# Deformable-convolution sampling: the subtraction for the low part of the coefficients goes from VectorE to GpSimd, behind its tap six

## What is computed

```
off, mask = projections of a depthwise convolution      # per pixel, 8 groups x 9 points
value     = x @ vp_w.T + vp_b
sampled   = bilinear reads of value at (pixel + point + off)
out       = sum over the 9 points of mask * sampled     # per group of 16 channels
x         = x + out @ op_w.T
```

## Time and profile before

| what | value |
|---|---|
| time, median of 3 runs | 1475.63 us (1475.12 to 1478.64) |
| the profiled execution | 1483.07 us, its span 1481.3 us |
| TensorE busy over the span | 81% |
| VectorE busy over the span | 66% |
| ScalarE busy over the span | 51% |
| GpSimd busy over the span | 48% |
| mean granted TensorE clock | 0.901 |

### The profile page before, as it was taken

One profiled execution on the slowest core, in us unless ns is written; L12 is line 12 of the kernel. 1 busy time (PEld: TensorE's weight loads), 2 busy tenths in 40 slices (PEclk: granted clock), 3 DMA queues, 4 the chain that ended last, 5 costly groups with the idle time before them and its releaser, 6 DMA issues. The chain is left out here.

```text
span 1481.3 us, 41520 instructions
## 1 busy us (share of the span) xinstructions
PE 1193.9 (81%) x13483; PEld 782.1 (53%) x13484; DVE 974.0 (66%) x2318; ACT 753.3 (51%) x1960; POOL 703.6 (48%) x842
## 2 busy tenths in 40 slices
PE   3982699999999987789887888887841699999974
PEld 1541344444444432355655555555530599999973
DVE  4996898888898732366777776767626244444435
ACT  1222555554555416367675665666410377777750
POOL 2000478787887850001144354454657355555550
PEclk9996699999999989699999998999755699999995
DMA  3000000000000012121112121221201122222218
GB/s 125 0 0 12 1 1 1 0 0 0 0 0 0 1 28 87 37 48 39 35 40 53 49 54 36 66 55 33 82 27 50 45 67 68 67 68 68 68 55 334
DMA packets 67555, 66.63 MB, mean 45 GB/s; under 512 B 13135, under 2 KB 57167, under 8 KB 67175
## 3 DMA queue, kind: packets, MB, share of 16 engines
q1 hardware_dynamic: 56679, 43.14, 10.8%
q0 software_dynamic: 8448, 17.58, 3.6%
q10 hardware_dynamic: 2304, 4.20, 0.7%
HBM read 29.93 MB, written 23.00 MB: 36 GB/s over the span
## 5 line engine op out<-in xcount | busy, mean ns | idle before, releaser
L1627 ACT ACTIVATE a_E<-a_E,a_nm 128x96 f32<-128x96 f32 x512 | 148.5, 364 | 117.8 <-DVE a_nm L1768 117.3
L2128 ACT ACTIVATE e_hT<-e_ph,e_b 128x128 f32<-128x128 f32 x544 | 155.5, 369 | 74.1 <-PE e_ph L2085 74.1
L441 POOL TENSOR_TENSOR s_pc<-s_wide,VP 128x512 f32<-128x512 f32 x112 | 143.0, 1277 | 74.8 <-ACT s_wide L520 68.8
L674 PE MATMUL s_pbc<-s_AT,s_sel 120*128 120x512 bf16 x400 | 134.2, 386 | 31.7 <-ACT s_wide L520 16.9
L432 POOL TENSOR_TENSOR s_acc<-s_acc,s_pb 128x512 f32<-128x512 f32 x112 | 142.3, 1270 | 22.0 <-DVE s_pb L603 21.5
L685 PE MATMUL s_pout<-s_pa,s_opT 128*128 128x512 f32 x288 | 151.5, 607 | 0.0
L2096 PE MATMUL e_py<-e_shared,e_hT 128*128 x1088 | 150.4, 281 | 1.1 <-ACT e_hT L2128 1.1
L2085 PE MATMUL e_ph<-e_xT,e_w1s 128*128 128x128 f32 x1088 | 147.7, 280 | 0.5 <-DVE e_w1s L2157 0.4
L1386 POOL DMA_INDIRECT slots<-m_pay,m_pos x128 | 128.2, 1002 | 38.8 <-issue 38.4
L2066 POOL DMA_INDIRECT picks<-e_yw,e_rows x136 | 134.3, 987 | 22.6 <-POOL e_tick L2064 21.0
L2085 PEld LDWEIGHTS e_ph<-e_xT,e_w1s 128*128 128x128 f32 x1088 | 134.6, 195 | 1.9 <-issue 0.9
(11 more groups left out here) (228 smaller groups left out, 2436.0 us busy)
## 6 DMA issues: line engine op xcount, KB each, us to landing
a_V<-a_VT SPq DMA_DIRECT2D x176, 68.0 KB
e_rows<-slots SPq DMA_DIRECT2D x136, 66.0 KB, 1.8
c_y<-picks SPq DMA_DIRECT2D x16, 512.0 KB, 5.6
X<-in_x SPq DMA_DIRECT2D x8, 512.0 KB, 8.1
out<-c_o ACTq DMA_DIRECT2D x16, 256.0 KB, 5.4
picks<-e_yw,e_rows POOLq DMA_INDIRECT x136, 2.3
e_w<-in_w SPq DMA_DIRECT2D x1, 2048.0 KB, 7.4
slots<-m_pay,m_pos POOLq DMA_INDIRECT x128
```

Of the source, the lines that this page charges most:

```text
L441: nc.gpsimd.tensor_tensor(prod_c[k][:].rearrange("p (a b) -> p a b", a=HALF), wide[k][:].rearrange("p (a b) -> p a b", a=HALF), window(n, ...
L674: pe.matmul(p_bc[bank_of["spread", t]][:], sel[:, t % 5, :], AT[j][:, t // 5, :], start=True, stop=True).then_inc(bc, 1)
L1627: act.activation(E[t % 2][:, o, :], E[t % 2][:, o, :], ACT.Exp, bias=nm[:, t % 2, o:o + 1]).then_inc(powered, 1)
L2128: ins = act.activation(hT[j % 2][:, q, :], p_h[j % 2][:, q * P:(q + 1) * P], ACT.Gelu, bias=b1[:, bass.ds(e, 1), q:q + 1].rearrange("p o h ...
```

## The change

GpSimd makes the subtraction `split_low` instead of VectorE. In its queue it stands behind tap 6, that is behind b6 and ahead of c8. The one for chunk 0 stands ahead of all chunks on GpSimd. VectorE's next `split_rest`, which overwrites `s_rest`, gets a wait for `low` of the chunk before. Nothing else moves: `low` still releases TensorE's round 0 behind tap 8.

```diff
             def _(pool):
                 nc.gpsimd.memset(zero[:], 0.0).then_inc(zeroed, 1)
 
+                def split_low(c):
+                    pool.wait_ge(mid, c + 1)
+                    nc.gpsimd.tensor_tensor(parts[:, :, :, 2].rearrange("p t a w -> p a t w"), rest[:],
+                                            parts[:, :, :, 1].rearrange("p t a w -> p a t w"), ALU.subtract)\
+                      .then_inc(low, 1)
+
                 def chunk(c, j, n):
...
                                 window(n, j, t), ALU.mult).then_inc(mul_c, 1)
+                        if t == 6 and (not known(c) or c + 1 < NCH):
+                            split_low(c + 1)
+                split_low(0)
                 chunks(pool, chunk)
...
-                def split_low(c):
-                    dve.wait_ge(mid, c + 1)
-                    dve.tensor_tensor(parts[:, :, :, 2].rearrange("p t a w -> p a t w"), rest[:],
-                                      parts[:, :, :, 1].rearrange("p t a w -> p a t w"), ALU.subtract)\
-                       .then_inc(low, 1)
-
...
                             if t == 1:
+                                dve.wait_ge(low, c + 1)
                                 split_rest(c + 1)
-                            if t == 5:
-                                split_low(c + 1)
...
                 split_rest(0)
-                split_low(0)
                 for k in range(WEIGHT_STEPS):
                     weights(1, k)
```

## The result

The changed kernel is slower: 1491.44 us median of 5 runs (1487.31 to 1519.86) against 1476.03 us, a ratio of 1.0085 with a 95% interval of 1.0058 to 1.0112, some 12.5 us.

A forecast was written before the change was run, and what follows sets the result against it. The prediction took a chunk's period as TensorE's work plus one place where VectorE is late. It added 17 us of longer chunks and 9 us of clock, 26 us, for about 1501 us median, range 1485 to 1517.

The forecast's parts named there:

- Where it stands: GpSimd's queue: subtraction behind c5 and b6, so round 0 starts 3.2 us later, old waits vanish; chunk about 1.0 us longer.
- The duration: The subtraction of 800 elements on GpSimd, priced from two-input f32 additions: 1.95 us.
- the two old waits: TensorE's waits at the spreads of taps 10 and 11: said to vanish, giving back 2.2 us a chunk.
- The removed contention: VectorE loses its 1.18 us subtraction; `s_MY` moves once b3 ends, and c5 takes 1.27 us, not 1.90.
- Chunk 14: The chunk without old waits, as it builds no coefficients: round 0 starts 2.2 us later than before.
- ahead of chunk 0: The first subtraction takes 1.95 instead of 0.99 us after its release, delaying the first products by 1.0 us.
- The sum without the clock: Sampling stage: 14 chunks at 1.0 us, plus 2.2 and 1.0 us, in all 17 us longer.
- The clock: TensorE at half clock behind the 14 stalls: 9.5 falls of 1.5 us instead of 3 of 1.7, 9 us more.
- the first rival: The stall at round 0 without more falls of the clock: 17 us longer, 1493 us; chance 0.18.
- one long piece is worse than two short ones: At round 0, by the skill page alone, one 3.2 us stall brings the clock down more than the two old waits.
- The rival "not slower": GpSimd's subtraction ends in time, taking at most 0.9 us: 1477 us, or 1472 without the three falls; chance 0.05.
- The rival of the full relief: VectorE's relief counts in full if round 0 does not wait: 2.2 us a chunk gone, 1445 us; chance 0.02.

The follow-up runs named there:

- the duplicate on VectorE: The filled kernel with 15 instead of 12 extra spreads, VectorE also making the subtraction at tap 5 into an unread tile: 1495.06 us, ratio 1.0119.
- the filled kernel: The changed kernel with 12 extra spreads of no use on TensorE ahead of its wait at round 0: 1487.51 us, ratio 1.0075.

## Why the prediction was right, and where it was off

- **Where it stands.** This was right, and it is the main mechanism: TensorE waits at round 0 and is released by GpSimd, the waits at taps 10 and 11 are gone, and c5, b6 and the subtraction follow each other without a gap. Moving the subtraction by one instruction moved the chunk by that instruction, and doubling it moved the chunk by its length.
- **The duration**, 1.95 us by f32 additions, was mis-sized: 1.70 us. This is 0.25 of the 0.4 us by which the stand, 2.8 us, is shorter than the 3.2 said. A chunk is 0.8 to 0.9 us longer (24.25 to 24.3 against 23.4), not 1.0, so the two old waits were worth 1.9 to 2.0 us instead of 2.2. For 14 chunks that is 11 to 12 us in place of 14.
- **The removed contention.** `s_MY` behind b3 and c5 at 1.27 us came as said; the duplicate on VectorE brought the 1.90 back and cost 0.5 to 0.6 us a chunk, where 0.63 was said. The Trainium skill's rule (SBUF — State Buffer, Who interferes with whom), that the instruction which started first keeps the other out, agrees with the trace: `s_MY` at 1.75 us ends 0.9 us behind b3.
- **Chunk 14** waits 1.68 us (said 2.2), and ahead of chunk 0 the first product is about 0.7 us later (said 1.0). The sum without the clock was 17 us; with the measured sizes it is about 14 us, and the filled kernel's stage, with the falls of before taken out, gives 15.
- **The clock** is the term whose form was wrong. I had 9.5 falls of 1.5 us each, as if every stand drew anew: 9 us in every execution. What the runs showed in its place is that falls repeat: once a fall begins within the stand, the chunk takes 27.3 us, 3.0 more, and the next stand meets the same, chunk after chunk, until the loop ends. Why the next stand meets it again is not shown. The time then depends on when this begins: at 395 us in the profile of 1504.33 us, at 248 us in those of 1517.37 and 1519.86. Six of the 17 executions end between 1487 and 1495 us, close to the first rival's 1493, and eleven between 1503 and 1529.
- **Luck in the number.** That the five executions of the result have a median of 1491 is chance, as three of the five are short ones; over all 17 it is 1511.5. Both lie in the range of 1485 to 1517, but my 1501 lies between the two kinds, where only the executions of 1503 and 1504 come near it.
- **What brings a fall.** The rule of the Trainium skill (TensorE: Matmul & The Clock Gate, The HAM clock gate), that idleness brings the clock down, agrees: 1.43 us of standing left it at 1.00, and 2.8 us did not. That one long piece is worse than two short ones, as I took from it, is not shown: the two waits of before, 1.86 us in all, had three falls in the loop, and single stands of 1.43 and 1.57 us had none.
- **The rival "not slower"** needed a duration of 0.9 us; it took 1.70.
- **The rival of the full relief** was priced at 1445 us, 2.2 us a chunk. Leaving the subtraction out showed 1460: VectorE's relief was worth 0.8 us, as tap 11's wait was shorter by only 0.1 us. With the subtraction ahead of c5 the trace shows what can stand behind that wait, the `s_PR` chain and ScalarE's order. In the change it did not matter, because the stand at round 0 covered it.

## What to carry to other kernels

Work that is moved to an engine with idle time takes the place in that engine's queue that it is given: ask when its result is due, count what stands ahead of it there, and put it just behind its input (here two instructions earlier turned +0.85% into -1.2%). A wait of TensorE is priced twice, by its length and by what the clock does behind it. Repeated in a loop, a long stand can lock into the dear form, so that executions of one kernel differ by 2 to 3%; then the median of a few says little. To tell the two prices apart, fill the stand with work that nobody uses.

## What was not expected of the hardware

- In a loop the falls of the clock fell into step: in one profile, from 395 us on, each chunk was 27.29 us long with about 6.8 us at half clock. Six spreads of filler (1.3 us) ended it.
- GpSimd takes 1.27 us to add two f32 operands of 512 elements and 1.52 us to subtract 800 elements of one tile from themselves, only 0.25 us for 288 more.
- A GpSimd instruction that meets VectorE's two-operand one is held up by it: where the subtraction stood ahead of c5, it took 2.52 us instead of 1.70, begun while `s_MY` (1.75 us) was under way. It was the better place all the same. The timeline of that kernel with its last placings moved by one tap:

```profile
301.33 1.75 DVE L558 TENSOR_TENSOR s_MY<-s_fac,OM 128x864 f32<-128x864 f32 x1
...
302.12 2.52 POOL L419 TENSOR_TENSOR s_parts<-s_rest,s_parts 128x800 bf16<-128x800 f32 x1
```
